# Cross-attention: both copies of the attended values out of PSUM on Vector, behind its first maximum of a step, in place of Scalar

## The reference

```python
x = _layernorm(x + attn(x))                 # causal self-attention with rotary positions, 16 heads
x = _layernorm(x + xattn(x, ctx, ctx, gamma))
x = _layernorm(x + ffn(x))                  # rms norm, 8-bit activations, ternary weights, 512 -> 2048 -> 512
...
def xattn(q, k, v, gamma):                  # 8 heads; the 128 rows are cut into 8 heads of 16, the 512 features are the positions
    qk = jnp.einsum('bhdq,bhdl->bhql', qh, kh) * scale      # 512 x 512 for each head, depth 16
    sm = jax.nn.softmax(qk, axis=-1)
    ret = jnp.einsum('bhql,bhdl->bhdq', sm, vh)
    return gamma * ret
```

## Time and profile before

| | |
|---|---|
| median of 3 runs | 1829.21 us |
| the profiled execution's time | 1833.27 us |
| its span, first to last instruction | 1831.5 us |
| mean granted clock of TensorE | 0.935 of 2.4 GHz |
| cross-attention, first to last copy of attended values | 625.4 to 1310.45 us |
| busy over the span: TensorE, Vector, Scalar, POOL | 88%, 84%, 75%, 52% |

### The profile page before, as it was taken

One profiled execution on the slowest core, in us unless ns is written; L12 is line 12 of the kernel. 1 busy time (PEld: TensorE's weight loads), 2 busy tenths in 40 slices (PEclk: granted clock), 3 DMA queues, 4 the chain that ended last, 5 costly groups with the idle time before them and its releaser, 6 DMA issues.

```text
span 1831.5 us, 35203 instructions
## 1 busy us (share of the span) xinstructions
PE 1609.7 (88%) x11936; PEld 873.5 (48%) x12000; DVE 1546.8 (84%) x2086; ACT 1377.0 (75%) x2853; POOL 961.4 (52%) x1408
## 2 busy tenths in 40 slices
PE   6999999999998889999999999999777777767774
PEld 4777777777775333333333333333233333333331
DVE  5788888888887989999989899999489999899985
ACT  4666645555453578888888888888699999899994
POOL 6667667676674533355544555323445555545542
PEclk9999999999999799999999999999878888888886
DMA  3465443434337454444464654444333333333311
GB/s 136 147 183 175 127 120 112 136 105 130 115 117 189 109 105 112 108 118 120 108 175 131 168 120 118 108 118 104 118 98 104 104 105 104 104 104 104 104 47 35
DMA packets 119269, 217.10 MB, mean 119 GB/s; under 512 B 32241, under 2 KB 34705, under 8 KB 116785
## 3 DMA queue, kind: packets, MB, share of 16 engines
q1 hardware_dynamic: 110770, 213.64, 41.5%
q0 software_dynamic: 8320, 1.21, 0.4%
HBM read 137.67 MB, written 76.02 MB: 117 GB/s over the span
## 4 chain that ended last, share of the span: by engine, by line
PE 58%; issue 12%; DVE 10%; ACT 7%; DMA 6%; POOL 5%; SPq 1%; POOLq 0%; DVEq 0%; ACTq 0%
PE sums L1059 13%; PE bank L1076 12%; PE bank L549 11%; PE wide L1029 6%; PE sums L549 5%; DMA out<-c_result 3%; PE wide L599 3%; DVE stage L1710 2%; ACT stage L1595 2%; PE wide L591 2%; ACT b_prob L945 2%; DVE a_prob L469 2%; PE sums L611 2%; DMA b_xs<-b_max_part 2%; PE wide L586 1%
## 5 line engine op out<-in xcount | busy, mean ns | idle before, releaser
L969 DVE TENSOR_REDUCE b_smax<-wide 128x2 f32<-128x1024 f32 x512 | 620.5, 1225 | 60.4 <-PE wide L1029 48.6
L945 ACT ACTIVATE b_prob<-bank 128x512 f32<-128x512 f32 x1024 | 556.3, 599 | 111.6 <-PE bank L1076 101.1
L1076 PE MATMUL bank<-b_xs,b_cs 50*128 50x512 f32 x1024 | 329.5, 478 | 23.6 <-ACT b_prob L945 13.2
L1059 PE MATMUL sums<-b_prob,b_vT 128*32 128x256 f32 (+1 forms) x3584 | 318.8, 428 | 5.2 <-ACT b_prob L945 0.5
L1029 PE MATMUL wide<-b_cs,b_xs 48*128 48x512 f32 x1024 | 282.8, 436 | 9.1 <-DVE b_smax L969 7.6
L1888 PE MATMUL sums<-c_w,c_hqT 128*128 128x512 bf16 x481 | 170.2, 530 | 114.1 <-issue 106.8
L1076 PEld LDWEIGHTS bank<-b_xs,b_cs 50*128 50x128 f32 x1024 | 133.4, 187 | 234.4 <-ACT b_prob L945 172.6
L885 POOL TENSOR_SCALAR b_max_part<-b_neg_max 16x128 fp32r<-16x128 f32 x64 | 18.6, 291 | 322.6 <-ACT b_neg_max L936 322.5
L370 ACT ACTIVATE a_prob<-wide,a_neg_max 128x128 f32<-128x128 f32 x512 | 181.8, 417 | 3.9 <-DVE a_neg_max L461 3.9
L1888 PEld LDWEIGHTS sums<-c_w,c_hqT 128*128 128x128 bf16 x512 | 63.4, 128 | 210.8 <-issue 185.9
L895 POOL DMA_DIRECT2D b_xs<-b_max_part x256 | 134.2, 530 | 42.1 <-POOL b_max_part L888 37.3
(11 more groups left out here) (147 smaller groups left out, 3247.7 us busy)
## 6 DMA issues: line engine op xcount, KB each, us to landing
scratch_c_part<-a_c_part SPq DMA_DIRECT2D x64, 256.0 KB
scratch_x_part<-a_x_part SPq DMA_DIRECT2D x64, 256.0 KB
b_xs<-scratch_x_part SPq DMA_DIRECT2D x128, 128.0 KB, 3.1
b_cs<-scratch_c_part SPq DMA_DIRECT2D x128, 128.0 KB, 3.1
scratch_heads<-b_heads SPq DMA_DIRECT2D x64, 256.0 KB, 2.6
a_xT<-in_xT SPq DMA_DIRECT2D x32, 256.0 KB, 6.4
a_c_in<-in_ctx SPq DMA_DIRECT2D x32, 256.0 KB, 2.6
a_x<-in_x SPq DMA_DIRECT2D x32, 256.0 KB, 4.1
```

Source lines behind the costliest of these rows:

```text
L945: act.activation(prob[k % 8][:, :], e_ps[bank_of(k)][:, :], ACT.Exp, scale=0.25).then_inc(exp_done, 1)
L969: dve.tensor_reduce(smax[g][:, :, j, qc], m_ps[u % 2][:, :, :], AX.X, ALU.max, negate=True).then_inc(max_done, 1)
L1059: last = pe.matmul(av_ps[2 * XD * h:2 * XD * (h + 1), cols], vT[p][:, lc, XG * g + h, :], prob[(XG * n + 2 * j + e) % 8][:, cols], start=( ...
L1076: pe.matmul(e_ps[bank_of(2 * u + e)][:, :], cs[p][g][half(e), j, lc * P:(lc + 1) * P], xs[p][g][half(e), j, :], start=True, stop=True).the ...
```

## The change

`copy_heads` moves from `scalar` to `vector` and becomes a `tensor_copy`; its waits and its semaphore stay the same. It stands behind the first of the two maxima of steps 1 and 5. The copies that fall into the last batch, in which Vector has no maxima, come at the end of Vector's cross-attention part (batch 30, group 1) and behind the feed-forward steps 1 and 2 (batch 31).

```diff
--- before.py
+++ after.py
@@ -923,19 +923,13 @@
         return begin, main
 
     def scalar(act):
-        def copy_heads(b, g, first=False):
-            act.wait_ge(av_done, STEPS * b + KC * (g + 1))
-            if not first:
-                act.wait_ge(heads_st[g], 16 * b)
-            act.activation(heads[g][:, :], av_ps[:, :], ACT.Copy).then_inc(heads_done, 1)
-
         def evict_max(b, g, first=False):
             act.wait_ge(mt_done, 2 * b + g + 1)
             if not first:
                 act.wait_ge(part_done, 4 * b + 2 * g - 2)
             act.activation(neg_max[g][:, :], m_ps[0][0:XG * KC, 0, 0:P], ACT.Copy).then_inc(neg_done, 1)
 
-        def step(t, first, second=False, last=False):
+        def step(t, first, last=False):
             for n in range(STEPS):
                 for j in range(XG):
                     k = XG * n + j
@@ -944,10 +938,6 @@
                         act.wait_ge(av_done, STEPS * t + n - 1)
                     act.activation(prob[k % 8][:, :], e_ps[bank_of(k)][:, :], ACT.Exp, scale=0.25).then_inc(
                         exp_done, 1)
-                    if j == 0 and n == 1 and not first:
-                        copy_heads(t - 1, 1, first=second)
-                    if j == 0 and n == 5:
-                        copy_heads(t, 0, first=first)
                 if n == 0:
                     evict_max(t, 1, first=first)
                 if n == 4 and not last:
@@ -955,11 +945,10 @@
 
         def pair(s, first, last):
             step(2 * s, first)
-            step(2 * s + 1, False, second=first, last=last)
+            step(2 * s + 1, False, last=last)
 
         evict_max(0, 0, first=True)
         pairs(act, pair)
-        copy_heads(NB - 1, 1)
 
     def vector(dve):
         def pair_max(b, u):
@@ -969,6 +958,12 @@
             dve.tensor_reduce(smax[g][:, :, j, qc], m_ps[u % 2][:, :, :], AX.X, ALU.max,
                               negate=True).then_inc(max_done, 1)
 
+        def copy_heads(b, g, first=False):
+            dve.wait_ge(av_done, STEPS * b + KC * (g + 1))
+            if not first:
+                dve.wait_ge(heads_st[g], 16 * b)
+            dve.tensor_copy(heads[g][:, :], av_ps[:, :]).then_inc(heads_done, 1)
+
         def reciprocals(b, first=False):
 
             dve.wait_ge(den_ld, 32 * b + 32)
@@ -988,9 +983,13 @@
             for n in range(STEPS):
                 if n == 5 and not first:
                     reciprocals(t - 1, first=second)
-                if not last:
-                    for j in range(2):
+                for j in range(2):
+                    if not last:
                         pair_max(t + 1, 2 * n + j)
+                    if j == 0 and n == 1 and not first:
+                        copy_heads(t - 1, 1, first=second)
+                    if j == 0 and n == 5 and not last:
+                        copy_heads(t, 0, first=first)
 
         def pair(s, first, last):
             step(s, 0, first, False, False)
@@ -1003,11 +1002,15 @@
             dve.wait_ge(rden_done, 1)
             dve.wait_ge(const_ld, 32)
             pairs(dve, pair, apart=(weights["of"].SCALE_PAIR,))
+            copy_heads(NB - 2, 1)
 
 
         def rest(t):
+            if t == 1:
+                copy_heads(NB - 1, 0)
             if t == 2:
                 reciprocals(NB - 2)
+                copy_heads(NB - 1, 1)
             if t == 6:
                 reciprocals(NB - 1)
```

## The result

The changed kernel takes **1942.84 us**, the median of four executions (1973.44, 1912.61, 1920.82, 1964.87; a fifth took 1944.76), against 1829.18 us for the kernel before on the same chip (1828.71 to 1835.35). The ratio is 1.047 with a 95% interval of 1.0417 to 1.0524. It is slower, as forecast, but the median lies 30 us above the range. The executions of one and the same changed kernel differ by 61 us; medians here are taken over all of them, ratios leave out those in which TensorE's clock was disturbed most, and that disturbance turns out to be part of the answer.

The account below looks back on a forecast made before the run. TensorE was taken to bound the cross-attention stage; 61 waits of 1.20 us (+73.2) less 5 us given back made +68 on 1833.3, so 1901.5 us for the profiled execution and 1897 us as median, range 1878 to 1913 us.

Parts of the forecast that it names:

- Where the time goes: Cross-attention stage: TensorE is the bound, 20.68 of 21.34 us a batch; Vector's work of 20.3 us still fits.
- Scalar's relief: Scalar gives up 0.48 us per copy, gaining nothing; as a rival, Scalar being the real bound, 1800 us, chance 3%.
- The new wait: Attended products behind 61 copies start at A + 1.92 instead of A + 0.72: 1.20 us later each, +73.2 us.
- A: The moment Vector's maximum in front of the copy starts, 1129.87 us in the earlier trace.
- the release: From the copy's end on Vector to TensorE's start of the attended products: taken as 0.10 us, between 0.05 and 0.15.
- The estimate of 0.74 us: Alternative price of Vector's copy from the skill page's PSUM access overheads; would make the sum 4 us higher.
- the row with 0.674: Profile row of Vector's plain copy of the same shape from PSUM, 0.674 us, used as the copy's price.
- TensorE does not catch up: Units behind a wait keep their 1.24 us pace, so all 1.20 us stays; rival of partial catching up, 1864 us, 5%.
- The give-back: Eight visible waits for the maxima's transfer, 14.5 us together, shrink by up to 1.20 us each: -5 us, at most 9.6.
- the 13.6 us of disturbances: Thirty batches before the change took 653.85 us against 640.2 at 21.34 us each; the excess was read as disturbances.
- The end of the stage: The three copies with no maximum in front, batch 30's second group and both of batch 31: nothing, plus or minus 1 us.
- the clock rival: TensorE's clock falls after the new waits, three units each at the low level: 170 us more, 2067 us; chance 4%.

Follow-up runs that it names:

- The kernel with the copies ahead: Changed kernel with both Vector copies moved ahead of the first maximum of steps 1 and 5 and the reciprocals: 1830.64 us, ratio 0.9959.
- the one with Scalar's late copies: Kernel before the change, with Scalar's two copies made two exponentials later: 2001.86 us, ratio 1.0676.
- the filled kernel: Changed kernel with TensorE repeating the last score four times ahead of the waiting attended products: 1907.87 us, ratio 1.0387; profiled span 1892.4 us.
- its sibling: Changed kernel with six repeats of the last score in each wait in place of four: 1897.5 us, ratio 1.0327.
- The four pairs of filled and unfilled kernels: Unfilled, then with repeated scores: changed kernel 1956.69, 1907.87 us; copies behind second maximum 2217.54, 2100.96; Scalar's late copies 2001.86, 1895.66; only group 1's copy on Vector 2023.91, 1881.48.
- The two filled kernels with the same 0.41 us of idle time per wait: Changed kernel with four repeated scores per wait, 1907.87 us; copies behind the second maximum with nine 50-row repeats, 2100.96 us.

## Why the prediction was right in direction and wrong in size

**Where the time goes: right.** TensorE bounds the stage and waits for the copy 61 times, Vector's busy time is no bound, Scalar's relief brings nothing worth naming. The kernel with the copies ahead shows the last two (0.9959 with the same load), the one with Scalar's late copies that the lateness alone does it.

**The new wait: right, 0.06 us short.** Forecast 1.20 us, measured 1.25 on the timeline and 1.265 over a batch. The copy started at A + 1.14 (1.15) and took 0.68 us (0.67), but the release took 0.15 us, what the earlier trace rows showed for Scalar, not the 0.10 I put between it and the earlier trace rows. 61 x 1.265 = 77.2 in place of 73.2. The estimate of 0.74 us by the Trainium skill's Perfetto Trace Analysis was too long for Vector's copy; the row with 0.674 was the better guide.

**TensorE does not catch up: right.** The products behind the wait follow each other as before, and Vector idles 0.80 us one maximum later (forecast 0.7).

**The give-back: too small.** I took 5 of the 13.6 us of disturbances. In the filled kernel, with no clock disturbance, thirty batches take 716.05 us, which is 30 x 23.87 to 0.1: all 13.6 came back, more than my bound of 9.6. The bound took it that each wait for the transfer shrinks by 1.20 us at most. Against eight waits, 14.5 us, the longest 4.8, the filled kernel has

```profile
PEld bank L1083 <- DMA b_xs<-b_max_part: 2.7, 4, 0.9
```

so the longest shrank by at least 3.9 us, and the stretches at the lower level that stood behind two of them in this part of the stage went with them. Why they shrank so far no run here shows. The end of the stage: 0.2 us less, forecast nothing plus or minus 1.

**The sum without the clock: right.** 77.2 - 13.6 = 63.6, so 1893 us by the corrected terms; the forecast was 1897, the filled kernel's profiled span of 1892.4 is a time of some 1894, and its sibling's median is 1897.5. The least disturbed execution of the changed kernel itself, 1905.75 us, is in the range.

**The step that failed: the clock rival, its chance of 4% and its shape.** The sum put the clock at nothing, because "the half with a stall of 1.10 us kept 1.00" and "the one comparable stall in this trace speaks against it". One stall could not show it, and it was not the only one. The same trace of the kernel before has three more stalls of TensorE of this length in the stage, each here with a stretch close behind it:

```profile
939.81 0.50 PE L1076 MATMUL bank<-b_xs,b_cs 50*128 50x512 f32 x2 [1.58 <-DMA b_xs<-b_max_part]
1040.75 0.50 PE L1076 MATMUL bank<-b_xs,b_cs 50*128 50x512 f32 x2 [1.47 <-DMA b_xs<-b_max_part]
1287.37 0.50 PE L1076 MATMUL bank<-b_xs,b_cs 50*128 50x512 f32 x2 [1.37 <-DMA b_xs<-b_max_part]
...
942.00:944.00 2.00, 2.00 (x15) 0.48 (x11) 1.23 (x1) 1.17 (x3) 0.00 (x0) 0.50 1.01 213
1042.00:1044.00 2.00, 1.98 (x21) 0.79 (x17) 1.99 (x3) 1.69 (x5) 0.20 (x1) 1.00 0.55 148
1290.00:1292.00 2.00, 1.74 (x9) 0.76 (x5) 0.00 (x0) 1.09 (x3) 0.74 (x2) 0.50 0.00 0
```

Of four stalls of 1.10 to 1.58 us, two (1.58 and 1.37) were followed by some microseconds at 0.50 and two (1.10 and 1.47) were not. The changed kernel adds 61 stalls of 1.3 us, so falls behind some of them were to be expected from the trace that I had. Of the 60 halves up to the 61st copy of its profiled execution 46 keep 1.00; the falls in the other 14 cost 70.5 us. And the rival was priced as all or nothing, each wait with three slow units (170 us), where the kernel did neither: some waits set off a long stretch at the lower level, worth about one to twelve episodes of 10.4 us per execution (1905.75 and 2018.85 us against 1894). The earlier trace rows had the price of that, units of 2.17 us instead of 1.24 for as long as it lasts; a case "some of the waits do it" with two to six episodes (21 to 62 us) would have reached from 1918 to 1959 and held the median. The Trainium skill, TensorE: Matmul & The Clock Gate, section "A second HAM failure mode: psum-queue depth-cycling", tells of frequent micro-idles between groups of matmuls that make the clock oscillate. The traces here agree: 1.33 us of idle time in front of 917.10, then 0.50. I had cited it and then outvoted it with a single row.

**What stays open.** Why a given wait sets off a fall and the next, equally long, does not; why two waits a batch have fewer than one; why three episodes of the profiled execution stand 14 halves apart. The four pairs of filled and unfilled kernels show that what TensorE does in the wait decides how often the clock falls. The two filled kernels with the same 0.41 us of idle time per wait, one without a fall and one with many, show that its length is not the whole of it. Whether the share of the array that works is the rest is not shown: a filling with 50 rows that leaves no idle time behind the second maximum, and one with 128 rows and 0.4 us left, were not tried. A copy whose lateness is spread over several short waits was not tried.

## What to carry to other kernels

Put a copy that frees a bank in front of long work on its engine, not behind it, where what it copies is ready that early: here the place in the queue was worth 4% by the ratios (1.0391 against 0.9959) and 7% in the median, the engine nothing. Where a change makes TensorE wait at regular places, cost the wait and then, as a case of its own with a price per episode, the clock. Look up every stall of that length in the trace at hand with the clock behind it, and do not take one undisturbed stall as proof. When the executions of a kernel scatter far more than those of the kernel before, compare them by mean clock first: here the scatter was a cost of the kernel and no noise.

## What I had not expected of the hardware

A wait of 1.1 to 1.3 us can be followed by 27 us and more at 1.2 GHz, and whether it is varies between executions of the same program. Fewer and shorter waits made it worse (2001.86 and 2023.91 us against 1942.84 and 1956.69). Useless matmuls in the wait won 49, 106, 117 and 142 us in the median (the last three between chips on which the kernel before differs by less than 1 us). And nine such matmuls on 50 rows of the array, with 0.41 us of idle time left, let the clock swing where nine on 128 rows, with 0.03 us left, held it at 1.00 in nearly the whole stage, 125 us apart.
